# Decoder layer on one core: where, in the last self-attention group, the key and value rounds' copies and subtractions and the row statistics of cross-attention are issued

## What is computed

```
x = x + attn(layernorm(x))             # scores = q k^T, p = relu(scores)^2, out = p v
x = x + xattn(layernorm(x), ctx, mask) # k = ctx Wk, v = ctx Wv, 16 heads of 64, softmax
x = x + ffn(layernorm(x))              # shared expert + one routed expert for each token
```

## Time and profile before

| what | value |
|---|---|
| runs | 2914.81 us median of 3 (2912.93 to 5002.09) |
| profiled execution | 2911.99 us, of it 2910.3 us span |
| mean granted TensorE clock | 0.992 |
| PE busy | 2789.2 us, 96% of the span |
| DVE, ACT, POOL busy | 62%, 55%, 36% |
| last self-attention group | about 662.6 to 825 us of the span |

### The profile page before, as it was taken

One profiled execution on the slowest core, in us unless ns is written; L12 is line 12 of the kernel. 1 busy time (PEld: TensorE's weight loads), 2 busy tenths in 40 slices (PEclk: granted clock), 3 DMA queues, 4 the chain that ended last, 5 costly groups with the idle time before them and its releaser, 6 DMA issues.

```text
span 2910.3 us, 46289 instructions
## 1 busy us (share of the span) xinstructions
PE 2789.2 (96%) x13287; PEld 2293.4 (79%) x13289; DVE 1808.6 (62%) x2744; ACT 1593.5 (55%) x2743; POOL 1060.5 (36%) x692
## 2 busy tenths in 40 slices
PE   7999999998889999999989999999999999999998
PEld 5888888886667888888867888887788888888886
DVE  6566665667476666666654434435876964776776
ACT  6888888886464555555531111111564743565665
POOL 6888888886431122222200000000133432332333
PEclk9999999999999999999999999999999999999999
DMA  1000000001220111111131211111986963876884
GB/s 62 26 26 11 25 29 25 25 11 55 80 66 29 44 32 51 37 40 43 60 120 39 69 68 58 58 58 47 326 308 246 347 242 121 291 284 220 289 287 178
DMA packets 190791, 322.70 MB, mean 111 GB/s; under 512 B 23528, under 2 KB 49128, under 8 KB 190720
## 3 DMA queue, kind: packets, MB, share of 16 engines
q1 hardware_dynamic: 179440, 296.61, 29.7%
q0 software_dynamic: 11280, 25.20, 2.6%
HBM read 286.86 MB, written 46.66 MB: 115 GB/s over the span
## 4 chain that ended last, share of the span: by engine, by line
PE 77%; issue 12%; DVE 5%; POOL 3%; ACT 3%; DMA 1%; POOLq 0%; DVEq 0%; SPq 0%; ACTq 0%
PE d_pG L1975 9%; PE d_pU L1975 9%; PE a_pS L47 4%; PE a_pS L49 4%; PE a_pS L48 4%; PE a_pO L47 3%; PE a_pO L49 3%; PE a_pO L48 3%; PE d_pD L49 3%; PE d_pD L47 3%; PE d_pD L48 3%; POOL b_S L700 2%; PE c_pD L47 2%; PE c_pD L49 2%; PE c_pD L48 2%
## 5 line engine op out<-in xcount | busy, mean ns | idle before, releaser
L157 POOL TENSOR_TENSOR a_pL<-a_p,a_pH 128x1024 fp32r<-128x1024 f32 x256 | 619.4, 2425 | 193.5 <-DVE a_p L348 191.7
L348 DVE TENSOR_TENSOR a_p<-a_r,a_pS 128x1024 f32<-128x1024 f32 x256 | 312.3, 1220 | 286.7 <-ACT a_r L165 279.6
L1231 DVE TENSOR_TENSOR e_wL<-e_raw,e_wH 128x1024 fp32r<-128x1024 f32 x384 | 450.2, 1217 | 34.9 <-PE d_pU L1975 24.7
L1226 ACT CAST e_wH<-e_raw 128x1024 fp32r<-128x1024 f32 x384 | 384.3, 1053 | 85.9 <-PE d_pD L49 59.5
L165 ACT ACTIVATE a_r<-a_pS 128x1024 f32<-128x1024 f32 x256 | 261.8, 1023 | 131.2 <-PE a_pS L49 129.5
L700 POOL TENSOR_TENSOR b_S<-b_S,b_ri 128x512 f32<-128x512 f32 x128 | 133.4, 1042 | 498.0 <-DVE b_ri L858 498.0
L165 ACT ACTIVATE a_pH<-a_r 128x1024 fp32r<-128x1024 f32 x256 | 271.9, 1062 | 9.1
L1467 POOL DMA_INDIRECT out<-d_og,c_iw x46 | 120.7, 2623 | 341.8 <-DVE d_og L1849 341.8
L47 PE MATMUL a_pS<-a_qH,a_kH 128*128 (+1 forms) x512 | 205.8, 402 | 6.7 <-DVE a_p L348 6.5
L717 ACT ACTIVATE b_S<-b_S,b_nm 128x128 f32<-128x128 f32 x512 | 198.4, 393 | 7.6 <-DVE b_nm L853 7.1
L47 PE MATMUL a_pO<-a_pH,a_vH 128*128 128x512 f32 x512 | 200.1, 391 | 1.5 <-POOL a_pL L157 1.5
(11 more groups left out here) (307 smaller groups left out, 7285.8 us busy)
## 6 DMA issues: line engine op xcount, KB each, us to landing
e_raw<-in_L_ffn_routed_gate_w SPq DMA_DIRECT2D x256, 256.0 KB
e_raw<-in_L_ffn_routed_up_w SPq DMA_DIRECT2D x256, 256.0 KB
e_raw<-in_L_ffn_routed_down_w SPq DMA_DIRECT2D x128, 512.0 KB
a_xb<-in_x SPq DMA_DIRECT2D x8, 1024.0 KB, 5.5
x<-a_base SPq DMA_DIRECT2D x32, 256.0 KB, 2.3
b_xr<-x SPq DMA_DIRECT2D x32, 256.0 KB, 3.5
x<-b_xr SPq DMA_DIRECT2D x32, 256.0 KB, 3.0
c_xb<-x SPq DMA_DIRECT2D x32, 256.0 KB, 3.0
```

What stands on the lines that cost most here:

```text
L157: nc.gpsimd.tensor_tensor(pL[:, j % RING, :, :], p[:, j % 2, :, :], pH[:, j % RING, :, :].bitcast(F32), ALU.subtract).then_inc(s["low"], 1)
L348: v.tensor_tensor(p[:, j % 2, :, :], r[:, j % 2, :, :], pS[j % 2][:, :, :], ALU.mult).then_inc(s["p"], 1)
L1226: copy(self.wH[n][:, :, :], self.raw[n][:, :, :]).then_inc(self.s["high"], 1)
L1231: unit.tensor_tensor(self.wL[n][:, :, :], self.raw[n][:, :, :], self.wH[n][:, :, :].bitcast(self.F32), self.sub).then_inc(self.s["low"], 1)
```

## The change

`late(j)` of PE, ACT and DVE is changed; no instruction is added or taken away except where they are issued.

- ACT's `k_high(n)` moves from the end of step `K_AT[n]` + 1 to the end of step `K_AT[n]`, DVE's `k_low(n)` from `K_AT[n]` + 2 to `K_AT[n]`; the same for `v_high` and `v_low`.
- The context transposes, copies and subtractions are all at the ends of steps 7 and 8 (before: PE 6 and 8, ACT 7 and 8, DVE 8 and 9).
- `row_scales` parts 0 to 6 move from steps 0 to 6 to steps 8, 10, 12, 14, 16, 18 and 20.

```diff
-    K_AT, V_AT = (9, 11, 13, 15), (17, 19, 21, 23)
+    C_AT, K_AT, V_AT = (7, 8), (9, 11, 13, 15), (17, 19, 21, 23)
+    SCALES_AT = (8, 10, 12, 14, 16, 18, 20)
...
         def late(j):
-            if j == 7:
-                c_high(0)
-            if j == 8:
-                c_high(1)
+            if j in C_AT:
+                c_high(C_AT.index(j))
             for n in range(PIECES):
-                if j == K_AT[n] + 1:
+                if j == K_AT[n]:
                     if n == 0:
                         act.wait_ge(s["zero"], 3)
                     k_high(n)
             for n in range(2 * NB):
-                if j == V_AT[n] + 1:
+                if j == V_AT[n]:
                     v_high(n)
...
         def late(j):
-            if j < 7:
-                if j == 0:
+            if j in SCALES_AT:
+                if j == SCALES_AT[0]:
                     dve.wait_ge(a["seen"], HEADS - NH - 1)
-                row_scales(j, 0, KNOWN - GT)
-            if j == 8:
-                c_low(0)
-            if j == 9:
-                c_low(1)
+                row_scales(SCALES_AT.index(j), 0, KNOWN - GT)
+            if j in C_AT:
+                c_low(C_AT.index(j))
             for n in range(PIECES):
-                if j == K_AT[n] + 2:
+                if j == K_AT[n]:
                     k_low(n)
             for n in range(2 * NB):
-                if j == V_AT[n] + 2:
+                if j == V_AT[n]:
                     if n == 0:
                         dve.wait_ge(s["zero"], 3 + 2 * NB)
                     v_low(n)
...
         def late(j):
-            if j == 6:
-                c_transpose(0)
-            if j == 8:
-                c_transpose(1)
+            if j in C_AT:
+                c_transpose(C_AT.index(j))
```

## The result

The changed kernel takes 2884.12 us (median of 4 runs, 2882.95 to 2884.25) beside 2915.09 us of the kernel before: 31.0 us less, a ratio of 0.9896 with a 95% interval of 0.9884 to 0.9908. Within 2%, as forecast, and 3 us from the forecast 2881. One of the four runs of before was disturbed and stands outside the ratio.

A forecast was written before the change was run, and what follows sets the result against it. PE, busy 96% of the span, was taken as the bound, so only its standstills could give time. Window gains of 33.5 us less 1.7 for clock gave 32, from 2911.99 to 2880, put 1 us up at 2881 (range 2877 to 2886).

The forecast's parts named there:

- step 5 to the end of `keys(0)`: First window, from 676.24 us: 18.8 us expected against 28.42, two small waits included, gain 9.6.
- three keys rounds: Steps 10 to 15: 25.5 us expected against 41.48, with no waits, gain 16.0.
- four values rounds, with the clock: Steps 16 to 23: 38.7 us against 45.13, waits of 5.2 included, gain 6.4, before 1.7 for the clock.
- behind step 23: After the last values round: `w_low` was to take 1.22 us instead of 3.00, ending a 1.52 us wait, gain 1.5.
- Rounds closed in their own step: Keys and values rounds: subtractions issued in the round's step end PE's wait for `b_k1L`, with 2.8 us to spare.
- T + 2.2: T is the end of PE's keys round; the relu behind copies and rounding was to start at T + 2.15.
- The statistics behind `a_p`: Steps 8 to 20: POOL lengthens the statistics, delaying `w_low`; new waits of 3.1 us at `new_values(0)`, 2.1 at `new_values(2)`.
- the one at `keys(0)`: Step 8: 1.60 us of aggregations ahead of `c_low(1)` make it end about 0.85 us late.
- The small wait of 0.2 us for scores of step 8: `w_low(0, 1)` in step 5, held by POOL, was to push `a_p` of step 6 past the need by 0.2 us.
- with the chain at its short price the waits are 0.9 and 0: Lower bound of the two values-round waits, if three small statistics instructions take 0.2 us each.
- The clock: After the two new waits: each low-clock stretch costs 1.7 us, 0 to 3.4 in all; one stretch was taken.
- Nothing behind the group changes: Nothing after the group depends on absolute time; a changed length behind 825 us would mean the forecast is wrong.

The follow-up runs named there:

- one step of lag: The changed kernel with copies and subtractions of keys and values one step after their round instead of in its own step: 2894.99 us, ratio 0.993.
- product in PSUM: The changed kernel with the temporary of the statistics in steps 16 and 20 kept in free bank `a_pX` instead of SBUF: 2880.69 us, ratio 0.9885.
- statistics last: The changed kernel with `row_scales` behind `c_low`, `k_low`, `v_low` and `w_low` in each step instead of ahead of them: 2874.11 us, ratio 0.9862.
- rounds alone: The changed kernel with the statistics put back at steps 0 to 6, context rounds still moved: 2881.48 us, ratio 0.9887.

## Why the prediction was right, and where it was off

| window (before) | gain forecast | measured |
|---|---|---|
| step 5 to the end of `keys(0)` | 9.6 | 28.42 - 19.01 = 9.4 |
| three keys rounds | 16.0 | 41.48 - 25.51 = 16.0 |
| four values rounds, with the clock | 6.4 - 1.7 = 4.7 | 45.13 - 41.76 = 3.4 |
| behind step 23 | 1.5 | 33.60 - 32.73 = 0.9 |
| group | 31.8 | 29.6 |

- **Rounds closed in their own step**: right, and most of the gain. The copies of the fourth keys round start at 721.62, 0.2 us behind PE's end at 721.42. The relu, which stands behind them and the rounding of weights, starts at 723.63, T + 2.2 as worked out. With one step of lag the waits came within 0.7 us of those counted by the same rule.
- **The statistics behind `a_p`**: right. The two waits were put at 3.1 and 2.1 us and are 2.87 and 1.95; the one at `keys(0)` at 0.85 and is 0.70. The small wait of 0.2 us for scores of step 8 did not come. The bound "with the chain at its short price the waits are 0.9 and 0" was wrong: with the chain at its short price they are 2.45 and 1.50, since `w_low` then meets POOL. I had taken that `w_low` costs 1.22 us when POOL is idle, and had not asked whether POOL is idle 2.2 us earlier.
- **The clock**: mis-sized. I took one stretch at the low level, 1.7 us; both waits were followed by one. The windows over the two rounds (columns as above) have a granted clock of 0.60, so that most of them ran at the lower of the two levels (1.2 and 2.4 GHz):

```profile
730.00:734.30 4.30, 4.30 (x12) 3.40 (x13) 1.00 (x1) 0.00 (x0) 2.37 (x1) 0.60 0.23 84
750.60:754.90 4.30, 4.30 (x12) 3.40 (x13) 1.61 (x2) 0.00 (x0) 2.38 (x1) 0.60 0.21 61
```

  From the start of the values round to the next scores it is 734.36 - 729.92 = 4.4 us at the first and 754.99 - 750.54 = 4.4 at the second, instead of 2.84: 1.6 us each, 3.2 in all, near the upper end of the 0 to 3.4 that I had given for it.
- **Behind step 23**: mis-sized, 0.9 for 1.5. The `w_low` of step 25 is indeed 1.22 us now, but it is the norm behind it that meets POOL, and PE still waits 0.62 us for `a_p`:

```profile
769.89 1.22 DVE L817 TENSOR_TENSOR b_wL<-b_raw_w,b_wH 128x1024 fp32r<-128x1024 f32 x1
771.02 2.63 DVE L825 TENSOR_SCALAR b_xn<-b_x,b_mv,b_rstd 128x512 f32<-128x512 f32 x1
```

  This is the same mistake as with the bound above.
- **Nothing behind the group changes**: not quite, and a change there was named as a sign of being wrong. From the first query on the span has 2086.69 us against 2085.43. These 1.26 us all lie in the last 911, in the feed-forward layer; the group also starts 0.66 us later. 29.6 - 1.3 - 0.7 is the 27.7 us between the two spans. Runs of one kernel differ by more than this: those of before lie between 2912.2 and 2917.6, which also is why the medians are 31.0 apart and the profiled executions 27.7. That 31.0 came so near to the forecast 32 is in part luck of this kind: window by window the forecast was 2.2 us too high. No experiment looked at the 1.3 us.

## What to carry to other kernels

When one buffer is handed round PE, ACT and DVE, put each engine's part as early in its own program as its input allows, and count from the end of the filling when the buffer is wanted again: the margin, not the load of the engine, tells whether a lag costs the filling engine; but a delay that the bank does not feel is carried on to the next result that is awaited. Where VectorE and GpSimd both work in SBUF, ask for each VectorE instruction who starts first; the one whose result is awaited belongs right behind the instruction that releases GpSimd, and small ones without a reader behind it. Moving work into an interval that is idle on average can cost more than it frees: here the statistics' move gave 6.4 us in one window and took 8.3 in another until its order inside the step was changed.

## What the runs showed of the hardware that was not expected

The price of a POOL subtraction passes on: the hold appeared at the 128x24 product (2.36 instead of 0.18), at `w_low` (2.96 instead of 1.22), at the norm (2.63 instead of 0.54) or, with DVE first, at POOL itself (3.31 instead of 2.4), by order alone. Two operands in SBUF are not the only way into it. In step 12 of the change POOL subtracts from 709.29 us on for 2.40, and an instruction that reads a single 128x24 operand is held as long; the next of its kind takes 0.18 us:

```profile
709.33 2.40 DVE L926 TENSOR_SCALAR b_tmp<-b_var 128x24 int32<-128x24 int32 x1
711.76 0.18 DVE L927 TENSOR_SCALAR b_rstd<-b_tmp 128x24 int32<-128x24 int32 x1
```

The 12 aggregations and `a_p`, which reads one operand in PSUM, ran beside POOL at their usual 1.60 and 1.22 us.

The length of a wait alone did not decide whether the clock fell. Behind waits of 1.95 and 2.87 us (the change) and 2.45 (product in PSUM) the next round ran low; behind one of 1.50 in the latter kernel, behind one of 1.95 with one step of lag (2.95 us from the round's start to the next scores; a keys round at full clock has 2.93), and behind two of over 2.5 us in the kernel before, among them the one shown by its clock of 1.00 in the earlier trace rows, it did not. What else decides it these runs don't show. In the two kernels without a wait at their keys and values rounds (statistics last, and rounds alone) the granted clock was 1.00 in both windows behind `keys(0)`; with the rounds alone it was 0.93 in the window before, where waits for `a_p` of up to 1.98 us are.
